# Weights times values in alternating column halves, and a 448/576 split of the subtraction, in a four-layer kernel

## Chip, core and metric

The kernel runs on one core of a Trainium2 chip. The metric is the device time of one execution in microseconds (us), as a median over several executions. The core has a matrix engine (TensorE, PE in the profile, with its weight loads in a row of their own, PEld), VectorE (DVE), ScalarE (ACT), GpSimd (POOL), and SyncE (SP), which issues DMAs. They run side by side and meet only at semaphores.

## The reference

Four layers act one after the other on x of shape (4, 1024, 128): a Mamba block, a mixture of experts, a differential attention, and a block with masked attention and experts. Only the third layer is touched. Per batch b it computes, for 8 heads with 64 value columns each:

```
dots = einsum('bhqd,bhkd->bhqk', q, k)          # 16 score maps, D = 32, two per head
attn_w = softmax(dots)
attn_w = attn_w[:, :, 0] - lam * attn_w[:, :, 1]  # one difference per head
attn = einsum('bhqk,bhkd->bhqd', attn_w, v)       # 64 value columns per head
attn = gamma * (attn / (rms + EPS)) * (1.0 - LAMBDA_INIT)
return attn.reshape(B, T, 512) @ Wout
```

T is 1024, so each head has two 1024x1024 maps in each of the 4 batches.

## The kernel before

The attention stage works in 256 units. Unit n is one block of 128 queries of one head: `unit(n)` gives batch b (64 units each), head group g (two heads, 16 units), query block i, and pp, which of the two heads. Two neighbouring units are a pair: the same queries, two heads. A pair's result is one 128x128 tile.

For one unit, two score maps of 128x1024 are made (`scores` with s = 0 and 1). On PE each is two f16 matmuls (L932) into a PSUM tile of its own, ps[0] or ps[1]. DVE takes the row maximum (L1090), and ACT the exponential with its row sum (L1017), into an SBUF buffer `P_of(n, s)`. The PSUM tile is then free for the next unit's map of the same s: PE waits for `a_ex(n - 1, s)`. Once a pair, `sums` makes the coefficients of the subtraction: a reciprocal on DVE (L1094), then two small POOL steps (L1147, L1151). `difference` computes z * coefficient + a in place: columns 0 to W on DVE (L1099), the others on POOL in two steps (L1156 multiply, L1159 add). W is 640 of 1024. `flip` transposes the difference in 8 chunks on PE (L943) into ps[2], and ACT copies it to SBUF as `DT[n % 2]` (L1024). `weigh` multiplies it by the values: 8 chunks, each with weights of 128x64 and a moving tile of 128x128 in f32 (L954), summed in PSUM partitions 64*pp to 64*pp + 64 of bank 6. PE executes each f32 product as two loads and two matmuls, so one `weigh` is 16 of each in the profile. When both heads of a pair are done, ACT copies the bank out (`gather`, L1030) and PE transposes it (`settle`, L960); DVE scales it (L1107).

All engines walk through one list, `ORDER`, made by `attention_order()`: its loop over n gives for each "slot" n what is put in line, and each engine takes what concerns it, in that order, never out of turn. Into these slots two more kinds of work are laid. Preparing pieces make the operands of the next head group (`op`: L914 on PE, L996 on ACT, L1084 on DVE; `v`: L919, L1004; `turn`, `norm`). Tail pieces `a0` to `a4` finish a batch whose last head group is being settled: root mean square (L1166, L1171 to L1175 on POOL, L1114 to L1123 on DVE) and output projection (L965 and L973 on PE). A batch's tail runs while the next batch's units go on. SP issues the DMAs that stack the operands (L892).

Of the kernel before, what the change touches and what calls it, by code (L numbers as in the profile page):

```python
# [8 lines left out]
F32 = mybir.dt.float32  # L9
# [3 lines left out]
ALU = mybir.AluOpType  # L13
ACT = mybir.ActivationFunctionType
# [90 lines left out]
def program(nc, d, out):  # L105
    ctx = ExitStack()
    with ctx:
# [16 lines left out]
        SEL = sb("sel", [128, 4096], BF16)  # L124
# [588 lines left out]

        N_UNITS, TL, W = 256, 4, 640
        s_wa, s_stack = sem("s_wa"), [[sem(f"s_stack{i}{j}") for j in range(2)] for i in range(2)]

        def unit(n):
            return n // 64, n // 16 % 4, n // 2 % 8, n % 2

        def attention_order():  # L720
# [47 lines left out]

            for n in range(N_UNITS + 8):
                if 0 <= n - 6 < N_UNITS and n % 2:  # L770
                    order.append(("gather", n - 6))
                if n < N_UNITS:
# [9 lines left out]
                if n < N_UNITS:  # L782
                    order.append(("scores", n, 1))
                if 0 <= n - 7 < N_UNITS and n % 2 == 0:
                    order.append(("settle", n - 7))
                    b, g, i, pp = unit(n - 7)
# [20 lines left out]
        t_axt, t_aop, t_av = tick("t_axt", NB, 2), tick("t_aop", NB, 4, 2, 2), tick("t_av", NB, 4, 2)  # L807
        t_as, t_at, t_aw, t_az = tick("t_as", N_UNITS, 2), tick("t_at", N_UNITS), tick("t_aw", N_UNITS), tick("t_az", PAIRS)
        t_a3, t_a4 = tick("t_a3", NB, 8), tick("t_a4", NB, 8)
# [6 lines left out]
        v_a1, v_a2 = tick("v_a1", NB, 8), tick("v_a2", NB, 8)  # L816
        p_ac, p_ad = tick("p_ac", PAIRS), tick("p_ad", N_UNITS)
        p_asq, p_arb, p_ax = tick("p_asq", NB, 8), tick("p_arb", NB, 8), tick("p_ax", NB)
# [31 lines left out]
        def ap2(x):  # L850
# [6 lines left out]
        V = [WB[:, 2048 + 1024 * i:3072 + 1024 * i].rearrange("p (j n) -> p j n", j=8) for i in range(2)]  # L857
        P_ = ([WB[:, 6144 + 1024 * i:7168 + 1024 * i] for i in range(3)] + [MA[:, 1024 * i:1024 * i + 1024] for i in range(3)]
              + [SEL[:, 2048 * i:2048 * i + 2048].bitcast(F32) for i in range(2)] + [WB[:, 5120:6144], BC[:, 0:2048].bitcast(F32)])
# [35 lines left out]
        def attention_pe(e):  # L895
            e.wait_ge(phase, 4)
            for p in ORDER:
# [37 lines left out]
                elif kind == "flip":  # L935
# [4 lines left out]
                    for k in range(8):  # L940
                        if 128 * k == W:
                            e.wait_ge(*p_ad.at(n))
                        x = e.transpose(ps[2][:, 128 * k:128 * k + 128], P_of(n, 0)[:, 128 * k:128 * k + 128], ident[:, :])  # L943
                    x.then_inc(*t_at.up(n))
                elif kind == "weigh":
                    n = p[1]
                    b, g, i, pp = unit(n)
                    e.wait_ge(*a_at.at(n))
                    if i == pp == 0:
                        e.wait_ge(*a_av.at(b, g, 1))  # L950
                    if pp == 0 and n:
                        e.wait_ge(*a_ag.at(n // 2 - 1))
# [23 lines left out]
        def attention_act(e):  # L976
# [3 lines left out]
            for p in ORDER:  # L980
# [17 lines left out]
                elif kind == "v":  # L998
# [3 lines left out]
                    if q >= 2 and h == 0:  # L1002
                        e.wait_ge(*t_aw.at(16 * q - 17))
                    e.activation(V[q % 2][:, 4 * h:4 * h + 4, :], bk.rearrange("p (j n) -> p j n", j=4), ACT.Copy,  # L1004
                                 scale=1.0).then_inc(*a_av.up(b, g, h))
                elif kind == "scores":
                    _, n, s = p
                    pp = n % 2
                    e.wait_ge(*v_amx.at(n, s))
                    if n >= 5:  # L1010
                        if s == 0:
                            e.wait_ge(*t_at.at(n - 5))
                        else:
                            e.wait_ge(*v_ad.at(n - 5))
                            e.wait_ge(*p_ad.at(n - 5))
                    L = L_of(n)
                    e.activation(P_of(n, s), ps[s][:, :], ACT.Exp, bias=L[:, 2 * s + pp:2 * s + pp + 1], scale=1.0,  # L1017
                                 accum_out=L[:, 4 + 2 * s + pp:5 + 2 * s + pp]).then_inc(*a_ex.up(n, s))
                elif kind == "flip":
                    n = p[1]  # L1020
                    e.wait_ge(*t_at.at(n))
                    if n >= 2:
                        e.wait_ge(*t_aw.at(n - 2))
                    e.activation(DT[n % 2], ps[2][:, :], ACT.Copy, scale=1.0).then_inc(*a_at.up(n))  # L1024
                elif kind == "gather":
                    m = p[1] // 2
                    e.wait_ge(*t_aw.at(2 * m + 1))
                    if m >= 2:
# [15 lines left out]
        def attention_dve(e):  # L1044
# [12 lines left out]
            for p in ORDER:  # L1057
# [33 lines left out]
                elif kind == "sums":  # L1091
                    n = p[1]
                    e.wait_ge(*a_ex.at(n, 1))
                    e.reciprocal(L_of(n)[:, 8:12], L_of(n)[:, 4:8]).then_inc(*v_ar.up(n // 2))  # L1094
                elif kind == "difference":
                    n = p[1]
                    e.wait_ge(*p_ac.at(n // 2))
                    a, z = P_of(n, 0), P_of(n, 1)
# [36 lines left out]
        def attention_pool(e):  # L1135
            e.wait_ge(phase, 4)
            for p in ORDER:
                kind = p[0]
                if kind == "norm" and p[2] == 1:
                    b = p[1]  # L1140
                    e.wait_ge(*v_ast[0].at(b))
                    rstd(e, st["m"]).then_inc(*p_ars[0].up(b))
                elif kind == "sums":
                    n = p[1]
                    L = L_of(n)
                    e.wait_ge(*v_ar.at(n // 2))
                    e.tensor_tensor(L[:, 12:14], L[:, 4:6], L[:, 10:12], ALU.mult).then_inc(*pool_own.up())  # L1147
                    if n == 1:
                        e.wait_ge(*v_lam.at(2))
                    e.wait_ge(*pool_own.now())  # L1150
                    e.tensor_scalar(L[:, 14:16], L[:, 12:14], lsc[:, 5:6], None, ALU.mult).then_inc(*p_ac.up(n // 2))  # L1151
                elif kind == "difference":
                    n = p[1]
                    a, z = P_of(n, 0), P_of(n, 1)
                    e.wait_ge(*p_ac.at(n // 2))
                    e.tensor_scalar(z[:, W:1024], z[:, W:1024], L_of(n)[:, 14 + n % 2:15 + n % 2], None, ALU.mult).then_inc(  # L1156
# [693 lines left out]
```

## Time and profile before

| | us |
|---|---|
| median of 3 runs (lowest to highest) | 3175.75 (3171.67 to 3178.06) |
| the profiled execution, its own time | 3170.2 |
| its span in the trace | 3168.4 |
| PE busy in the span | 2407.0 (76%) |
| DVE busy | 2311.8 (73%) |
| ACT busy | 1678.5 (53%) |
| POOL busy | 1263.5 (40%) |

The busy shares are over the whole program. The attention stage, from about 1289 us to 2500 us of the span, is a good third of it and has its own shares, which the rows below give by stretch. Matmul durations include the time through the array, so neighbouring ones overlap, and the distance between starts says more than a duration.

### The profile page before, as it was taken

How to read it: one execution, taken by the hardware profiler on the slowest of the kernel's cores; microseconds unless marked ns; L12 is line 12 of the kernel's file. 1: busy time of each engine (PE TensorE's matmuls, PEld its weight loads, DVE VectorE, ACT ScalarE, POOL GpSimd, SP SyncE). 2: the span in 40 equal slices, each digit the busy share in tenths (PEclk: the TensorE clock that was granted, in tenths of full speed). 3: DMA queues.
4: the chain of work that ended last, by engine and by line, in shares of the span. 5: the costliest groups of instructions: out<-in, count | busy, mean ns of one | idle time of the engine just before them, and what ended most of it. 6: DMA issues, size and time to landing. Idle time of an engine off the chain costs nothing.

```text
span 3168.4 us, 41094 instructions
## 1 busy us (share of the span) xinstructions
PE 2407.0 (76%) x14962; PEld 1690.2 (53%) x14962; DVE 2311.8 (73%) x4141; ACT 1678.5 (53%) x2552; POOL 1263.5 (40%) x1203
## 2 busy tenths in 40 slices
PE   3114776667676696899999999999999388667867
PEld 1002444344344564577777777776777366245635
DVE  3994798699599612688878878887888533874386
ACT  4223663665376242678777877787778124022402
POOL 0341143144124200365766576667667540114011
PEclk8556878888788898799999999999999789788978
DMA  3000000000000000100000100010000100000000
GB/s 99 0 0 0 0 1 1 1 1 1 1 1 1 1 1 14 41 21 21 24 21 21 28 21 21 24 29 21 21 21 1 40 1 1 0 14 1 1 0 14
DMA packets 32026, 41.96 MB, mean 13 GB/s; under 512 B 8897, under 2 KB 18130, under 8 KB 31442
## 3 DMA queue, kind: packets, MB, share of 16 engines
q1 hardware_dynamic: 31826, 39.34, 4.6%
q8 instruction: 120, 1.97, 0.3%
q14 instruction: 80, 0.66, 0.1%
HBM read 12.05 MB, written 2.10 MB: 4 GB/s over the span
## 4 chain that ended last, share of the span: by engine, by line
PE 46%; DVE 20%; issue 18%; POOL 11%; ACT 4%; SPq 1%; DMA 1%; POOLq 0%; DVEq 0%; ACTq 0%
PE ps L954 10%; PE ps L932 6%; PE ps L943 6%; POOL MA L379 5%; PE ps L710 3%; DVE MA L1090 3%; DVE MA L1410 3%; PE ps L914 2%; DVE lnb L265 2%; PE ps L1724 2%; PE ps L645 2%; PE ps L1711 2%; PE ps L647 1%; PE ps L646 1%; PE ps L1648 1%
## 5 line engine op out<-in xcount | busy, mean ns | idle before, releaser
L1090 DVE TENSOR_REDUCE MA<-ps 128x1 f32<-128x1024 f32 x512 | 623.1, 1220 | 190.4 <-PE ps L932 177.6
L379 POOL TENSOR_TENSOR MA<-MA,BIG 128x1024 f32<-128x1024 f32 x120 | 280.1, 2355 | 624.3 <-DVE BIG L350 624.3
L954 PE MATMUL ps<-MA,WB 128*64 128x128 f32 x4096 | 504.5, 277 | 0.0
L954 PEld LDWEIGHTS ps<-MA,WB 128*64 128x64 f32 x4096 | 442.8, 137 | 88.4 <-issue 87.4
L344 DVE TENSOR_TENSOR_SCAN BIG<-BIG 128x1024 f32<-128x1024 f32 x128 | 346.8, 2748 | 0.0
L932 PE MATMUL ps<-BIG 96*128 96x512 f16 x1024 | 312.6, 387 | 13.3 <-DMA BIG<-WB 4.9
L632 ACT ACTIVATE HR<-ps,b 128x512 f32<-128x512 f32 x288 | 191.5, 686 | 244.0 <-PE ps L647 243.0
L710 PEld LDWEIGHTS ps<-WB,HR 128*128 128x128 f32 x2304 | 305.8, 209 | 25.0 <-issue 8.7
L710 PE MATMUL ps<-WB,HR 128*128 128x128 f32 x2304 | 312.8, 294 | 0.0
L1017 ACT ACTIVATE WB<-ps,MA 128x1024 f32<-128x1024 f32 x206 | 229.5, 1114 | 149.3 <-DVE MA L1090 147.5
L497 PE MATMUL ps<-bc,sel 96*128 96x512 bf16 x256 | 108.2, 520 | 249.1 <-DVE BIG L350 190.7
L1024 ACT ACTIVATE MA<-ps 128x1024 f32<-128x1024 f32 x256 | 259.8, 1015 | 4.9 <-PE ps L943 4.9
L436 ACT ACTIVATE BIG<-MA,aneg 128x1024 f32<-128x1024 f32 x128 | 141.5, 1142 | 109.9 <-DVE BIG L344 105.8
L1017 ACT ACTIVATE MA<-ps,MA 128x1024 f32<-128x1024 f32 x153 | 170.6, 1115 | 44.8 <-DVE MA L1090 44.8
L497 PEld LDWEIGHTS ps<-bc,sel 96*128 96x128 bf16 x256 | 22.2, 113 | 302.2 <-DVE BIG L350 213.0
L1147 POOL TENSOR_TENSOR MA<-MA 128x2 f32<-128x2 f32 x128 | 25.0, 195 | 365.2 <-DVE MA L1094 365.2
L943 PE MATMUL ps<-ident,WB 128*128 128x128 f32 x1232 | 166.1, 279 | 5.6 <-POOL WB L1159 2.5
L943 PEld LDWEIGHTS ps<-ident,WB 128*128 128x128 f32 x1232 | 144.4, 144 | 44.4 <-DVE WB L1099 10.8
L645 PE MATMUL ps<-xT,WB 128*128 128x512 f16 x288 | 126.5, 439 | 52.4 <-ACT HR L632 48.3
L248 POOL TENSOR_SCALAR st_d<-st_d 128x8 f32<-128x8 f32 x16 | 4.3, 269 | 402.6 <-DVE st_d L260 402.5
L589 DVE SCALAR_TENSOR_TENSOR acc<-ps,g,acc 128x128 f32<-128x128 f32 x256 | 71.0, 337 | 123.2 <-PE ps L710 123.2
L340 DVE TENSOR_TENSOR BIG<-MA,ps 128x1024 f32<-128x1024 f32 x128 | 149.6, 1207 | 1.2 <-PE ps L497 1.2
(286 smaller groups left out, 5133.2 us busy)
## 6 DMA issues: line engine op xcount, KB each, us to landing
BIG<-BIG SPq DMA_DIRECT2D x192, 64.0 KB, 2.0
BIG<-WB SPq DMA_DIRECT2D x192, 64.0 KB, 2.0
WB<-w_dram SPq DMA_DIRECT2D x1, 2304.0 KB, 14.6
X<-x_dram SPq DMA_DIRECT2D x4, 512.0 KB, 12.5
HR<-w_dram SPq DMA_DIRECT2D x1, 2048.0 KB, 9.3
out_dram<-X SPq DMA_DIRECT2D x4, 512.0 KB, 3.2
WB<-wqkv_dram SPq DMA_DIRECT2D x1, 1536.0 KB, 6.1
WB<-w_dram SPq DMA_DIRECT2D x2, 512.0 KB, 8.2
```

The lines of the kernel that those rows point to most:

```text
L340: e.tensor_tensor(db[k][c], du[:, c, :], ps[0][:, :], ALU.mult).then_inc(*v_mtb.up(b, n, c))
L344: e.tensor_tensor_scan(db[k][c], da[k][c], db[k][c], 0.0, ALU.mult, ALU.add).then_inc(*v_mscan.up(b, n, c))
L379: e.tensor_tensor(yy[:, c, :], yy[:, c, :], db[n % 2][c], ALU.add).then_inc(*p_my.up(b, n, c))
L632: e.activation(hr[(4 * k + f) % 8], bank[4 + f % 2], ACT.Gelu, bias=small["b1"][:, PLAN[k][1], f:f + 1], scale=BACK).then_inc(*a_fg.up(b, ...
L645: e.matmul(o, w[0], x[0], start=first, stop=False)
L710: i = e.matmul(o, hr[(4 * kk + f) % 8][:, 128 * j:128 * j + 128], w2[:, x, f, :], start=f == 0 and x != 8, stop=f == 3)
L932: x = e.matmul(ps[s][:, 512 * h:512 * h + 512], stack[q % 2][0:96, 0, 2 * pp + s, 128 * i:128 * i + 128], stack[q % 2][0:96, 1, 2 * pp + s ...
L943: x = e.transpose(ps[2][:, 128 * k:128 * k + 128], P_of(n, 0)[:, 128 * k:128 * k + 128], ident[:, :])
L954: x = e.matmul(bank[6][64 * pp:64 * pp + 64, 0:128], V[(4 * b + g) % 2][:, k, 64 * pp:64 * pp + 64], DT[n % 2][:, 128 * k:128 * k + 128], ...
L1017: e.activation(P_of(n, s), ps[s][:, :], ACT.Exp, bias=L[:, 2 * s + pp:2 * s + pp + 1], scale=1.0, accum_out=L[:, 4 + 2 * s + pp:5 + 2 * s ...
L1024: e.activation(DT[n % 2], ps[2][:, :], ACT.Copy, scale=1.0).then_inc(*a_at.up(n))
L1090: e.tensor_reduce(L_of(n)[:, c:c + 1], ps[s][:, :], AX, ALU.max, negate=True).then_inc(*v_amx.up(n, s))
```

## The change

`weigh` no longer does one head after the other. It is now done for a pair in two pieces: piece 0 takes chunks 0 to 3 and piece 1 chunks 4 to 7, and within a piece each chunk is done for head 0 and then for head 1. The two heads' weights lie in different column halves of the array, and their results in different partitions of bank 6. Each piece still has 8 products (16 loads and 16 matmuls in the profile). Since a piece needs both heads' differences, it stands one or two slots later; `gather` and `settle` move one and two slots later, and `DT` has four buffers. These take over the memory of two of the ten P buffers; now the s = 0 maps have five and the s = 1 maps three, so the exponential of (n, 1) waits for the difference of n - 3 and no longer of n - 5. The subtraction is split at 448: DVE does 448 columns, POOL 576. The coefficients are made on DVE alone, the reciprocal and then one small fused step, which waits for the reciprocal by a semaphore.

```
-        N_UNITS, TL, W = 256, 4, 640
+        N_UNITS, TL, W = 256, 4, 448
...
-                if 0 <= n - 6 < N_UNITS and n % 2:
-                    order.append(("gather", n - 6))
+                if 0 <= n - 7 < N_UNITS and n % 2 == 0:
+                    order.append(("gather", n - 7))
...
-                if 0 <= n - 7 < N_UNITS and n % 2 == 0:
-                    order.append(("settle", n - 7))
+                if 0 <= n - 9 < N_UNITS and n % 2 == 0:
+                    order.append(("settle", n - 9))
...
-                if 0 <= n - TL - 1 < N_UNITS:
-                    order.append(("weigh", n - TL - 1))
+                if 0 <= n - 6 - n % 2 < N_UNITS:
+                    order.append(("weigh", (n - 6) // 2, n % 2))
...
-        DT = [MA[:, 3072 + 1024 * i:4096 + 1024 * i] for i in range(2)]
+        DT = ([MA[:, 3072 + 1024 * i:4096 + 1024 * i] for i in range(2)]
+              + [SEL[:, 2048 * i:2048 * i + 2048].bitcast(F32) for i in range(2)])
...
         def P_of(n, s):
-            return P_[(2 * n + s) % 10]
+            return P_[s][n % len(P_[s])]
...
-                    for k in range(8):
-                        x = e.matmul(bank[6][64 * pp:64 * pp + 64, 0:128], V[(4 * b + g) % 2][:, k, 64 * pp:64 * pp + 64],
-                                     DT[n % 2][:, 128 * k:128 * k + 128], start=k == 0, stop=k == 7)
-                    x.then_inc(*t_aw.up(n))
+                    for k in range(4 * half_, 4 * half_ + 4):
+                        for pp in range(2):
+                            x = e.matmul(bank[6][64 * pp:64 * pp + 64, 0:128], V[(4 * b + g) % 2][:, k, 64 * pp:64 * pp + 64],
+                                         DT[(2 * m + pp) % 4][:, 128 * k:128 * k + 128], start=k == 0, stop=k == 7)
+                    x.then_inc(*t_aw.up(m, half_))
...
-                    if n >= 5:
-                        if s == 0:
-                            e.wait_ge(*t_at.at(n - 5))
-                        else:
-                            e.wait_ge(*v_ad.at(n - 5))
-                            e.wait_ge(*p_ad.at(n - 5))
+                    if s == 0 and n >= 5:
+                        e.wait_ge(*t_at.at(n - 5))
+                    if s == 1 and n >= 3:
+                        e.wait_ge(*v_ad.at(n - 3))
+                        e.wait_ge(*p_ad.at(n - 3))
...
-                    e.reciprocal(L_of(n)[:, 8:12], L_of(n)[:, 4:8]).then_inc(*v_ar.up(n // 2))
+                    L = L_of(n)
+                    e.reciprocal(L[:, 8:12], L[:, 4:8]).then_inc(*v_ar.up(n // 2))
+                    if n == 1:
+                        e.wait_ge(*v_lam.at(2))
+                    e.wait_ge(*v_ar.at(n // 2))
+                    e.scalar_tensor_tensor(out=L[:, 14:16], in0=L[:, 4:6], scalar=lsc[:, 5:6], in1=L[:, 10:12], op0=ALU.mult,
+                                           op1=ALU.mult).then_inc(*v_ac.up(n // 2))
...
-                elif kind == "sums":
-                    n = p[1]
-                    L = L_of(n)
-                    e.wait_ge(*v_ar.at(n // 2))
-                    e.tensor_tensor(L[:, 12:14], L[:, 4:6], L[:, 10:12], ALU.mult).then_inc(*pool_own.up())
-                    if n == 1:
-                        e.wait_ge(*v_lam.at(2))
-                    e.wait_ge(*pool_own.now())
-                    e.tensor_scalar(L[:, 14:16], L[:, 12:14], lsc[:, 5:6], None, ALU.mult).then_inc(*p_ac.up(n // 2))
```

On PE, in two neighbouring slots in the middle of the stage, there stood this before (L932 scores, L943 flip, L960 settle, L954 weigh, x8 products):

```order
L932 MATMUL ps<-BIG 128x512 x2
L943 MATMUL ps<-ident,MA 128x128 x8
L932 MATMUL ps<-BIG 128x512 x2
L960 MATMUL ps<-ident,OS 128x128
L954 MATMUL ps<-MA,WB 64x128 x8
L932 MATMUL ps<-BIG 128x512 x2
L943 MATMUL ps<-ident,sel 128x128 x8
L932 MATMUL ps<-BIG 128x512 x2
L954 MATMUL ps<-MA,WB 64x128 x8
```

Now, with the lines moved by a few (L933, L944, L963, L957), and with a preparing piece (L915) in the row:

```order
L933 MATMUL ps<-BIG 128x512 x2
L944 MATMUL ps<-ident,bc 128x128 x8
L933 MATMUL ps<-BIG 128x512 x2
L963 MATMUL ps<-ident,OS 128x128
L957 MATMUL ps<-sel,WB 64x128 x8
L915 MATMUL ps<-xT,WB 128x512
L933 MATMUL ps<-BIG 128x512 x2
L944 MATMUL ps<-ident,WB 128x128 x8
L933 MATMUL ps<-BIG 128x512 x2
L957 MATMUL ps<-sel,WB 64x128 x8
```

The places of the weigh blocks between the scores are the same, and so is the count of 8 products in each; what is new is inside a block, where heads alternate. On DVE, one pair stood so before (L1090 maxima, L1094 reciprocal, L1107 scaling of a settled tile, L1099 difference):

```order
L1090 TENSOR_REDUCE MA<-ps 128x1
L1094 RECIPROCAL MA<-MA 128x4
L1090 TENSOR_REDUCE MA<-ps 128x1
L1107 TENSOR_TENSOR MA<-ps,MA 128x128
L1099 SCALAR_TENSOR_TENSOR WB<-WB,MA 128x640
L1090 TENSOR_REDUCE MA<-ps 128x1 x2
L1099 SCALAR_TENSOR_TENSOR WB<-MA,WB 128x640
```

and stands so now (L1092, L1097, L1115, L1107 in the same roles, L1101 the new small step):

```order
L1092 TENSOR_REDUCE MA<-ps 128x1
L1097 RECIPROCAL MA<-MA 128x4
L1101 SCALAR_TENSOR_TENSOR MA<-MA,lsc 128x2
L1092 TENSOR_REDUCE MA<-ps 128x1
L1115 TENSOR_TENSOR MA<-ps,MA 128x128
L1107 SCALAR_TENSOR_TENSOR WB<-MA,WB 128x448
L1092 TENSOR_REDUCE MA<-ps 128x1 x2
L1107 SCALAR_TENSOR_TENSOR bc<-MA,bc 128x448
```

One small step has come between the reciprocal and the second maximum, and the differences are narrower.

## Rows read from the trace of the kernel before

**Rows 1.** Busy time of each engine by stretch (us, and number of instructions)

```profile
1321.00:1530.00 209.00, 206.40 (x1470) 154.69 (x1469) 176.45 (x233) 171.37 (x288) 124.20 (x150) 1.00 0.10 25
...
1562.00:1634.00 72.00, 65.74 (x461) 50.72 (x460) 55.65 (x72) 51.85 (x90) 54.23 (x62) 0.98 0.09 23
1634.00:1732.00 98.00, 92.93 (x667) 71.51 (x665) 82.34 (x137) 72.25 (x126) 57.99 (x68) 1.00 0.07 17
1732.00:1828.00 96.00, 94.33 (x666) 70.53 (x667) 80.67 (x100) 80.47 (x136) 58.62 (x70) 1.00 0.12 28
```

**Rows 2.** Reciprocals (L1094, one a pair) in two stretches: DVE busy, number

```profile
1562.00:1634.00 72.00, 1.18 (x7) 0.98 0.09 23
1634.00:1732.00 98.00, 1.49 (x9) 1.00 0.07 17
```

**Rows 3.** The chain of waits from 1798 us: start, us, what

```profile
1800.04 1.89 PE ps L954 x16
1801.93 1.05 PE ps L914 x2
1802.98 0.43 PE ps L932 x2
1803.42 0.88 PE ps L943 x8
...
1806.62 0.54 PE ps L932 x2
...
1808.59 0.11 PE ps L960
```

**Rows 4.** Timeline of one pair: start, us, engine and instruction [idle before]

```profile
1799.96 1.23 DVE L1090 TENSOR_REDUCE MA<-ps 128x1 f32<-128x1024 f32 x1
1799.97 1.96 PE L954 MATMUL ps<-MA,WB 128*64 128x128 f32 x16
...
1803.46 2.53 DVE L1090 TENSOR_REDUCE MA<-ps 128x1 f32<-128x1024 f32 x2 [1.28 <-PE ps L932]
...
1804.71 1.11 ACT L1017 ACTIVATE WB<-ps,MA 128x1024 f32<-128x1024 f32 x1 [0.93 <-DVE MA L1090]
...
1805.82 1.02 ACT L1024 ACTIVATE MA<-ps 128x1024 f32<-128x1024 f32 x1
...
1806.72 1.11 ACT L1017 ACTIVATE WB<-ps,MA 128x1024 f32<-128x1024 f32 x1
...
1807.72 0.21 ACT L1017 ACTIVATION_READ_ACCUMULATOR WB<-ps,MA 128x1 f32 x1
...
1807.98 0.60 PE L932 MATMUL ps<-BIG 96*128 96x512 f16 x2
...
1808.63 1.23 DVE L1090 TENSOR_REDUCE MA<-ps 128x1 f32<-128x1024 f32 x1
```

**Rows 5.** Groups by shape, 1600 to 2200 us: busy us, mean ns, idle before

```profile
L954 PEld LDWEIGHTS ps<-MA,WB 128*64 128x64 f32 x2048 | 220.1, 137 | 44.4 <-issue 43.9
...
L1099 DVE SCALAR_TENSOR_TENSOR WB<-WB,MA 128x640 f32<-128x640 f32 x26 | 23.6, 906 | 2.7 <-POOL MA L1151 2.7
...
L914 PEld LDWEIGHTS ps<-xT,WB 128*128 128x128 f32 x64 | 9.5, 188 | 10.1 <-issue 4.8 <-DVE HR L1107 2.7 <-DVE MA L1107 2.7
```

**Rows 6.** POOL's groups by shape, 1828 to 1863 us (a batch's tail)

```profile
L1173 POOL TENSOR_TENSOR MA<-MA,half 128x8 f32<-128x8 f32 x3 | 5.5, 1837 | 0.2
L1166 POOL TENSOR_TENSOR MA<-HR 128x512 f32<-128x512 f32 x4 | 4.1, 1035 | 0.0
...
L1156 POOL TENSOR_SCALAR MA<-MA 128x384 f32<-128x384 f32 x2 | 2.5, 1242 | 0.1
...
L1159 POOL TENSOR_TENSOR MA<-MA 128x384 f32<-128x384 f32 x1 | 1.0, 998 | 0.1
...
L1151 POOL TENSOR_SCALAR MA<-MA,lsc 128x2 f32<-128x2 f32 x3 | 0.9, 296 | 0.3
L1147 POOL TENSOR_TENSOR MA<-MA 128x2 f32<-128x2 f32 x3 | 0.6, 197 | 2.3 <-DVE MA L1094 2.3
```

More of the change, by code:

```diff
@@ L767, in tail_piece @@
                     tails[0][2] = v
-            for n in range(N_UNITS + 8):
-                if 0 <= n - 6 < N_UNITS and n % 2:
-                    order.append(("gather", n - 6))
+            for n in range(N_UNITS + 11):
+                if 0 <= n - 7 < N_UNITS and n % 2 == 0:
+                    order.append(("gather", n - 7))
                 if n < N_UNITS:
@@ L783, in attention_order @@
                     order.append(("scores", n, 1))
-                if 0 <= n - 7 < N_UNITS and n % 2 == 0:
-                    order.append(("settle", n - 7))
-                    b, g, i, pp = unit(n - 7)
+                if 0 <= n - 9 < N_UNITS and n % 2 == 0:
+                    order.append(("settle", n - 9))
+                    b, g, i, pp = unit(n - 9)
                     if g == 3:
@@ L857, in program @@
         V = [WB[:, 2048 + 1024 * i:3072 + 1024 * i].rearrange("p (j n) -> p j n", j=8) for i in range(2)]
-        P_ = ([WB[:, 6144 + 1024 * i:7168 + 1024 * i] for i in range(3)] + [MA[:, 1024 * i:1024 * i + 1024] for i in range(3)]
-              + [SEL[:, 2048 * i:2048 * i + 2048].bitcast(F32) for i in range(2)] + [WB[:, 5120:6144], BC[:, 0:2048].bitcast(F32)])
+        P_ = [[WB[:, 6144 + 1024 * i:7168 + 1024 * i] for i in range(3)] + [WB[:, 5120:6144], BC[:, 0:2048].bitcast(F32)],
+              [MA[:, 1024 * i:1024 * i + 1024] for i in range(3)]]
         osl = [OS[:, 128 * i:128 * i + 128] for i in range(2)]
-        DT = [MA[:, 3072 + 1024 * i:4096 + 1024 * i] for i in range(2)]
+        DT = ([MA[:, 3072 + 1024 * i:4096 + 1024 * i] for i in range(2)]
+              + [SEL[:, 2048 * i:2048 * i + 2048].bitcast(F32) for i in range(2)])
         O_ = [MA[:, 5120:9216].rearrange("p (i n) -> p i n", i=8), HR[:, :].rearrange("p (i n) -> p i n", i=8)]
@@ L940, in attention_pe @@
                     for k in range(8):
-                        if 128 * k == W:
+                        if k == W // 128:
                             e.wait_ge(*p_ad.at(n))
@@ L945, in attention_pe @@
                 elif kind == "weigh":
-                    n = p[1]
[L947 to L952, printed above, removed]
-                    for k in range(8):
-                        x = e.matmul(bank[6][64 * pp:64 * pp + 64, 0:128], V[(4 * b + g) % 2][:, k, 64 * pp:64 * pp + 64],
-                                     DT[n % 2][:, 128 * k:128 * k + 128], start=k == 0, stop=k == 7)
-                    x.then_inc(*t_aw.up(n))
+                    _, m, half_ = p
+                    b, g, i, _ = unit(2 * m)
+                    if half_ == 0:
+                        e.wait_ge(*a_at.at(2 * m + 1))
+                        if i == 0:
+                            e.wait_ge(*a_av.at(b, g, 1))
+                        if m:
+                            e.wait_ge(*a_ag.at(m - 1))
+                    for k in range(4 * half_, 4 * half_ + 4):
[3 more added lines that the diff above has]
+                    x.then_inc(*t_aw.up(m, half_))
                 elif kind == "settle":
@@ L1002, in attention_act @@
                     if q >= 2 and h == 0:
-                        e.wait_ge(*t_aw.at(16 * q - 17))
+                        e.wait_ge(*t_aw.at(8 * q - 9, 1))
                     e.activation(V[q % 2][:, 4 * h:4 * h + 4, :], bk.rearrange("p (j n) -> p j n", j=4), ACT.Copy,
@@ L1021, in attention_act @@
                     e.wait_ge(*t_at.at(n))
-                    if n >= 2:
-                        e.wait_ge(*t_aw.at(n - 2))
-                    e.activation(DT[n % 2], ps[2][:, :], ACT.Copy, scale=1.0).then_inc(*a_at.up(n))
+                    if n >= 4:
+                        e.wait_ge(*t_aw.at(n // 2 - 2, 1))
+                    e.activation(DT[n % 4], ps[2][:, :], ACT.Copy, scale=1.0).then_inc(*a_at.up(n))
                 elif kind == "gather":
                     m = p[1] // 2
-                    e.wait_ge(*t_aw.at(2 * m + 1))
+                    e.wait_ge(*t_aw.at(m, 1))
                     if m >= 2:
```

9 lines of the change are left out of this document (4 added, 5 removed).

## The prediction

> **What bounds the kernel now.** I read the page's busy shares first, then only the attention stage, since nothing else is touched. Busy time by stretch [rows 1] shows PE at 206.4 of 209 us, at granted clock 1.00, in the first long regular stretch; DVE and ACT are at 84% and 82%, POOL at 59%. The stage has four sequences, one a batch. A batch's tail overlaps the next batch's start, and there no engine is full: 1562 to 1634 us has PE at 65.7 of 72, POOL at 54.2. The stretch after it, 1634 to 1732, is again near PE's limit, 92.9 of 98. The later sequences repeat this pattern, and the last has nothing left to prepare.
>
> The chain of waits [rows 3] says the same in detail. For pairs with a preparing piece it runs through PE without a gap: two weigh blocks of 1.89, one L914 of 1.05, scores of 0.43 and 0.54 twice each, two flips of 0.88, one settle of 0.11. The sum is 3.78 + 1.05 + 1.94 + 1.76 + 0.11 = 8.64 us, and the timeline [rows 4] has the second maximum of one pair at 1799.96 and of the next at 1808.63, 8.67 apart. So PE is full. But the same rows hold a second limit which is just as tight, and I think it decides this case. From the first maximum of the odd slot (1803.46) the work goes: exponential at 1804.71, the copy of the flip at 1805.82, the other exponential at 1806.72, its accumulator read until 1807.93, PE's scores at 1807.98, the second maximum at 1808.63. Every step starts as the one before it ends. These 5.17 us are a chain over DVE, ACT and PE that holds no weigh block.
>
> **The change, part by part.**
>
> *Weigh.* A block has 16 matmuls in 1.89 us, 0.118 each [rows 3]. A flip, with the full 128 columns of weights, takes 0.88 for 8, 0.110 each. So a product with 64 columns costs as much as one with 128: half the array stands idle. The trace of before holds no case of two column halves in neighbouring matmuls, so the overlap is to be bounded. Lower end: two halves fully side by side, 0.95 us. Upper end: none, 1.89. Between them I look at the loads. A load of 64 columns takes 137 ns and one of 128 columns 188 [rows 5], so 64 columns cost about 51 ns of streaming and the rest is latency; 16 loads in a row would need 0.82, less than 0.95, so loads alone don't forbid the overlap. But an engine that now wants two loads per matmul time has little spare, and some latency will show. I take 1.1 us, nearer the lower end, a choice: saving 0.79 per block.
>
> The Trainium skill, "TensorE: Matmul & The Clock Gate", section "Part 3: Packing small matmuls — row/col tiling", says that column tiles run at the same time and reports 2.38 times for three of them; by that ratio per tile (an estimate) two would give 1.59, a block of 1.19, and the total below would lose about 7 us of its gain. The same section says a load overlaps running matmuls only when the row group differs, which would speak against the change, since both halves use all rows. The trace disagrees for loads of one tile: the 137 ns loads fit 16 into a block of 1.89 us without adding to it.
>
> *What the saving is worth.* In an even slot the order is scores, flip, scores, settle, weigh, preparing piece, and then the next slot's scores; the rows of the order show that the change keeps this. From the second maximum at 1799.96 to the next slot's first at 1803.46 are 3.50 us, through the weigh block and L914; this part gets 0.79 shorter. Then comes the 5.17 chain, in which the second block of the pair is hidden. A pair with a preparing piece thus takes 3.50 − 0.79 + 5.17 = 7.88 instead of 8.67. The second block's saving is lost in this chain.
> A pair without one: PE's way would be 3.50 − 1.05 − 0.79 = 1.66, but DVE has a maximum, a settle scaling and a difference to do, some 2.0 us (1.23 as the row has it, and about 0.8 for the other two, narrowed). So 2.0 + 5.2 = 7.2, where PE's sum of before is 8.64 − 1.05 = 7.6 to 7.7; gain 0.5. In 8 pairs there are 6 with a piece (4 L914, 2 of L919): the mean gain is (6 × 0.79 + 2 × 0.5) / 8 = 0.72.
> Regular pairs: 209 us at 8.6 are 24 or 25, and each later sequence has 12 (96 us, [rows 1]); the last has about 7 pairs without any piece. 54 × 0.72 + 7 × 0.5 = 42 us. The stretch like 1634 to 1732 has 9 pairs [rows 2] and comes three times; it has output projections on PE besides, and I give it the same 0.72: 27 × 0.72 = 19 us. Together −61.
>
> *DVE.* The difference of 640 columns takes 0.906 mean [rows 5]; 192 fewer of 640 columns, if all but 0.2 scales, saves 0.2 twice a pair. The new small step with its wait for the reciprocal costs 0.15 to 0.3 (POOL's small steps take 0.2 and 0.3, [rows 6], and nearer rows there aren't). It sits between the two maxima, on the 5.17 chain's side branch. Net 0 to −0.2 per pair; I count 0. Behind that wait on DVE stands the second maximum, for which ACT waits, but ACT comes to it 2 us after the first.
>
> *POOL.* Each difference goes from 384 to 576 columns. Now 1.242 + 0.08 + 0.998 = 2.32 [rows 6]. With 0.2 fixed in each (the 2-column step takes 0.197) it becomes 1.76 + 0.08 + 1.40 = 3.24, in proportion 3.44. Per pair +1.8 to +2.2, and −0.75 for the two coefficient steps with their gaps. POOL then has about 6.5 to 6.9 per pair of 7.9: covered in regular stretches. The exponential of (n, 1) now waits for the difference of n − 3. Counted from the coefficients, the first difference is ready after 3.3 and wanted after about 6, the second after 6.6 and wanted after about 10: some 3 us of cover. If that cover goes, ACT stalls, and behind it the flip copies.
> In tails it is gone. There POOL also has 1.04 and 1.84 and two small steps, about 3.6 us with gaps per row block, next to each pair [rows 6]: 5.4 + 3.6 = 9.0 before, 6.5 + 3.6 = 10.1 and more after. About 12 pairs of each of three tails (4 before 1562, 7 in 1562 to 1634 [rows 2], and one) get 1.1 to 1.4 longer on POOL; POOL is 75% busy there, so I let half of it reach the end: 12 × 1.25 × 0.5 = 7.5, less 12 × 0.72 × 0.5 = 4.3 that PE gives: +3 each, +9, rounded to +8. The last tail has nothing to hide it: 4 pairs × 1.1, and it starts two slots later because settle moved: +12.
>
> *The rest.* The later gather, settle and V-buffer waits have whole slots of room; weigh of a pair waits for the second head's copy, made one slot before; SP's stacking is unchanged. Counted at 0; if the gather came late, PE's next first piece would stand, about 0.3 a pair.
>
> **The sum.** −61 + 8 + 12 = −41 us. The profiled execution has 3170.2 (span 3168.4), so 3129. It is 5.6 below the median of 3175.75; on the medians I forecast 3135 us.
>
> **The rivals.**
> *A, the chain loosens.* Overlap is full (0.95 to 1.0) and the 5.17 chain isn't binding, because a head start of one slot is carried along; the pair goes to what DVE needs, about 84% of 8.66, 7.2. Then 54 × 1.46 + 7 × 0.5 + 27 × 1.2 = 115, less 20 for tails: 3081. For it: DVE idles 1.28 before 1803.46. Against it: every start in the chain touches an end.
> *B, slower: the halves don't overlap.* PE runs products in turn whatever their columns, the block stays 1.89, and no regular pair gains. The tails pay in full: 12 × 1.25 × 0.5 × 3 = 22, and 12 at the end: 3175.75 + 34 = 3210. It decides from a block of about 1.63 us upwards, since the 61 us of gain shrink in proportion and 20 must be paid. The skill's sentence on row groups would be this case. For it: no row shows overlap; each matmul is paced by its 128 moving rows.
> *C, POOL takes the bound.* Its steps are stretched beside DVE's wider use of the same memory and take 4 us per difference: 8 us a pair. Then the regular pairs gain about 0.6, 88 × 0.6 = 53 in all, and the tails pay 12 × 2.4 × 0.5 × 3 = 43 and 18: 3184. For it: POOL's steps of one shape differ in length. Against: means are near the shortest.
>
> **Chances and range.** Forecast 0.48 (3105 to 3160), A 0.20, B 0.20, C 0.12. From them: faster by over 0.2% (what a measurement of this kernel can tell, about 6 us) 0.72, with a little of C; same 0.07; slower 0.21. The range runs from 3075, just under A, to 3200, which leaves out most of B: 3075 to 3200.
>
> **What would show it.** The weigh row: 16 matmuls in about 1.2 us, against 1.96. Steady pairs 7.9 apart with a piece and 7.2 without. PE no longer full, 85 to 90% in regular stretches. POOL at 576 columns 1.76 and 1.40, over 80% busy; ACT waiting for POOL only in tails, and the last stretch after the final unit longer. I am wrong if the block keeps its length, if starts in the 5.17 chain draw apart, or if ACT waits for L1159's successor in steady pairs.

## The result and the profile after

The changed kernel takes 3193.74 us in the median (3187.35 to 3198.83, five runs), the kernel before 3176.47 beside it (3171.67 to 3179.14): ratio 1.0055, 95% interval 1.0038 to 1.0071. It is slower by half a per cent, where I had forecast 3135. The profiled execution has a span of 3195.1, against 3168.4.

The page's busy rows and its chain, of the changed kernel:

```profile
PE 2257.7 (71%) x14962; PEld 1491.2 (47%) x14962; DVE 2346.0 (73%) x4269; ACT 1679.1 (53%) x2552; POOL 1426.6 (45%) x947
...
PE 32%; DVE 31%; issue 19%; POOL 12%; ACT 5%; SPq 1%; DMA 1%; POOLq 0%; ACTq 0%; DVEq 0%
```

PE is busy for 149 us less, yet the kernel is not faster. The stretches that answer to [rows 1] (PE, PEld, DVE, ACT, POOL busy, granted clock, DMA):

```profile
1321.00:1530.00 209.00, 174.36 (x1458) 112.71 (x1458) 182.95 (x254) 169.69 (x288) 153.12 (x98) 0.98 0.10 24
...
1562.00:1634.00 72.00, 56.83 (x470) 39.60 (x471) 57.31 (x81) 52.94 (x92) 65.72 (x50) 0.98 0.09 23
1634.00:1732.00 98.00, 78.38 (x630) 53.64 (x628) 83.54 (x127) 73.09 (x125) 73.05 (x50) 0.93 0.07 17
1732.00:1828.00 96.00, 78.17 (x632) 51.88 (x632) 79.42 (x121) 71.55 (x122) 67.48 (x43) 0.95 0.10 25
```

In the first stretch PE went from 206.4 to 174.4 of 209, and DVE from 176.5 to 183.0. The timeline of a steady pair with a preparing piece answers to [rows 4]:

```profile
1802.62 1.22 DVE L1092 TENSOR_REDUCE MA<-ps 128x1 f32<-128x1024 f32 x1
...
1802.63 1.09 PE L957 MATMUL ps<-sel,WB 128*64 128x128 f32 x16
...
1803.77 0.28 DVE L1115 TENSOR_TENSOR HR<-ps,MA 128x128 f32<-128x128 f32 x1
...
1804.10 1.12 PE L915 MATMUL ps<-xT,WB 128*128 128x512 f32 x2 [0.38 <-DVE HR L1115]
...
1805.70 2.53 DVE L1092 TENSOR_REDUCE MA<-ps 128x1 f32<-128x1024 f32 x2 [1.06 <-PE ps L933]
...
1807.69 1.40 POOL L1158 TENSOR_TENSOR WB<-WB,MA 128x576 f32<-128x576 f32 x1
...
1808.15 1.42 DVE L1107 SCALAR_TENSOR_TENSOR WB<-MA,WB 128x448 f32<-128x448 f32 x1
...
1811.56 1.22 DVE L1092 TENSOR_REDUCE MA<-ps 128x1 f32<-128x1024 f32 x1
```

Three things are to be seen. The weigh block has 16 matmuls in 1.09 us, where it had 1.96: the column halves do run side by side. PE then waits for DVE's L1115: the scaling of the settled tile reads bank 7, into which the preparing piece L915 is to write, and on DVE it stands behind a maximum of 1.22 us. And the difference L1107 of the odd slot takes 1.42 us for 448 columns, where 640 took 0.9; it begins while POOL's add L1158 runs and ends 0.48 after it. The chain of waits has both, and repeats every 9.06 us:

```profile
1811.64 1.13 DVE MA L1092
1812.78 0.21 DVE HR L1115
1812.98 0.04 issue
1813.03 1.12 PE ps L915 x2
1814.15 0.43 PE ps L933 x2
1814.59 0.88 PE ps L944 x8
1815.46 0.45 PE ps L933 x2
1815.91 0.02 issue
1815.93 1.23 DVE MA L1092
1817.16 1.47 DVE WB L1107
1818.63 0.60 DVE BIG L1086
1819.23 1.13 DVE MA L1092
```

No weigh block is left in it, and no step of ACT either. (I had written that the engines meet only at semaphores; these two steps, which no semaphore joins, show that VectorE and GpSimd do not.)

Where the time went by stretch is read from the reciprocals, one a pair. The 40th and the 52nd, which bound the middle of the second sequence, first of the kernel before, then of the changed one:

```profile
1642.96 0.17 DVE L1094 RECIPROCAL MA<-MA 128x4 f32<-128x4 f32 x1
...
1757.56 0.17 DVE L1094 RECIPROCAL MA<-MA 128x4 f32<-128x4 f32 x1
```

```profile
1642.27 0.16 DVE L1097 RECIPROCAL MA<-MA 128x4 f32<-128x4 f32 x1
...
1771.03 0.17 DVE L1097 RECIPROCAL MA<-MA 128x4 f32<-128x4 f32 x1
```

These 12 pairs went from 114.6 to 128.8 us. The same stretches of the third and fourth sequence lost 14.1 and 12.1, so 40 in all; everything else between the first and the last reciprocal gained 17.5 together; behind the last one 4.0 were lost. 40.4 − 17.5 + 4.0 is the 27 by which the spans differ.

The twelve pairs do not hold the same work in both kernels. Settle stands two slots later, and with it every tail piece of the batch: by `ORDER`, 15 tail pieces fall between these two reciprocals where there were 12, and 27 into the twelve pairs before them where there were 30. Those earlier pairs gained 3.8, 3.2 and 5.7 us in the three sequences. Of the 14.2, 14.1 and 12.1 lost, 9.6, 10.1 and 11.9 lie in the last three pairs, where the kernel before has no tail piece left.

Two more things are seen in the same stretch: what PE waited for (us in all, times, longest), and the busy times with the granted clock (the third number from the end), each first of the kernel before, then of the changed one:

```profile
PE ps L914 <- DVE HR L1107: 2.2, 2, 1.9
...
PE ps L973 <- DVE WB L1084: 0.8, 1, 0.8
```

```profile
1642.96:1757.56 114.60, 107.86 (x761) 81.45 (x760) 97.58 (x158) 86.66 (x149) 69.60 (x80) 1.00 0.09 22
```

```profile
PE ps L915 <- DVE HR L1115: 9.5, 8, 4.9
PE ps L976 <- DVE BIG L1086: 6.3, 3, 2.4
```

```profile
1642.27:1771.03 128.76, 99.87 (x774) 68.49 (x774) 105.77 (x172) 88.51 (x151) 88.73 (x60) 0.91 0.08 19
```

With the smaller rows, PE's waits for DVE at the spare bank were 4.6 us and are 21.0. Half of the 21.0 is not the wait for the scaling: the projection pieces of the tail (L968, L976) wait for L1086, DVE's last step of an odd slot, which stands behind the difference. And the granted clock, 1.00 before, is now 0.91 (0.91 and 0.90 in the other two sequences), so that part of the stretch ran at the lower of the two levels, 1.2 GHz. One such place, behind a wait of 3.02 us:

```profile
1715.81 1.03 PE L933 MATMUL ps<-BIG 96*128 96x512 f16 x2 [3.02 <-ACT bc L1019]
...
1719.53 1.98 PE L957 MATMUL ps<-MA,WB 128*64 128x128 f32 x16
```

The weigh block takes 1.98 there instead of 1.09. The PE steps that stand in the chain of waits at such lengths add up to some 8 to 10 us more than the same steps at clock 1.00 (an estimate, from the chain between these two reciprocals). No run holds the clock fixed, so what it is worth is not shown; e9 below loses 33 us in the three stretches at 0.97, so it is not the whole of the 40.

### The profile page after: what moved, and what is told of

Read it like the earlier page. It is cut to its first block, busy times and chain, and to the rows that moved or that the text cites. A ratio compares the mean times of both kernels' runs of the same rounds, so it can differ in the third digit from the quotient of the medians.

```text
span 3195.1 us, 40966 instructions
## 1 busy us (share of the span) xinstructions
PE 2257.7 (71%) x14962; PEld 1491.2 (47%) x14962; DVE 2346.0 (73%) x4269; ACT 1679.1 (53%) x2552; POOL 1426.6 (45%) x947
## 4 chain that ended last, share of the span: by engine, by line
PE 32%; DVE 31%; issue 19%; POOL 12%; ACT 5%; SPq 1%; DMA 1%; POOLq 0%; ACTq 0%; DVEq 0%
DVE MA L1092 10%; POOL MA L379 5%; PE ps L933 4%; PE ps L944 4%; PE ps L710 3%; DVE MA L1409 3%; DVE WB L1107 3%; POOL MA L1155 2%; PE ps L915 2%; DVE lnb L265 2%; PE ps L1723 2%; PE ps L645 2%; PE ps L1710 2%; PE ps L646 1%; PE ps L647 1%
## 5 line engine op out<-in xcount | busy, mean ns | idle before, releaser
L1092 DVE TENSOR_REDUCE MA<-ps 128x1 f32<-128x1024 f32 x512 | 623.1, 1220 | 189.0 <-PE ps L933 180.7
L1155 POOL TENSOR_SCALAR MA<-MA 128x576 f32<-128x576 f32 x256 | 454.3, 1775 | 257.8 <-DVE MA L1101 256.8
L933 PE MATMUL ps<-BIG 96*128 96x512 f16 x1024 | 325.0, 400 | 52.1 <-ACT WB L1019 31.5
L1158 POOL TENSOR_TENSOR WB<-WB,MA 128x576 f32<-128x576 f32 x205 | 293.1, 1430 | 17.1
L1019 ACT ACTIVATE MA<-ps,MA 128x1024 f32<-128x1024 f32 x256 | 286.2, 1118 | 22.9 <-POOL WB L1158 12.3
L944 PE MATMUL ps<-ident,WB 128*128 128x128 f32 x1640 | 233.1, 287 | 40.1 <-ACT MA L1026 12.5
L944 PEld LDWEIGHTS ps<-ident,WB 128*128 128x128 f32 x1640 | 197.7, 148 | 112.6 <-issue 48.2
L1107 DVE SCALAR_TENSOR_TENSOR WB<-MA,WB 128x448 f32<-128x448 f32 x205 | 188.5, 919 | 0.0
L933 PEld LDWEIGHTS ps<-BIG 96*128 96x128 f16 x1024 | 83.4, 101 | 146.7 <-ACT WB L1019 50.0
## 6 DMA issues: line engine op xcount, KB each, us to landing
X<-x_dram SPq DMA_DIRECT2D x4, 512.0 KB, 12.7
```

The lines of the kernel that those rows point to most:

```text
L933: x = e.matmul(ps[s][:, 512 * h:512 * h + 512], stack[q % 2][0:96, 0, 2 * pp + s, 128 * i:128 * i + 128], stack[q % 2][0:96, 1, 2 * pp + s ...
L1092: e.tensor_reduce(L_of(n)[:, c:c + 1], ps[s][:, :], AX, ALU.max, negate=True).then_inc(*v_amx.up(n, s))
L1107: e.scalar_tensor_tensor(out=a[:, 0:W], in0=z[:, 0:W], scalar=L_of(n)[:, 14 + n % 2:15 + n % 2], in1=a[:, 0:W], op0=ALU.mult, op1=ALU.add) ...
L1158: e.tensor_tensor(a[:, W:1024], a[:, W:1024], z[:, W:1024], ALU.add).then_inc(*p_ad.up(n))
```

## The experiments

Two theories. **Theory 1, the collision:** DVE's difference and POOL's add, which both read two operands in SBUF, hold each other up, and the change puts them beside each other. **Theory 2, the bank:** with a short weigh block PE waits for the scaling that frees the spare bank. A third was that POOL is simply overloaded. The clock and the moved tail pieces have no experiment of their own. Each kernel was timed beside the kernel before on the same chip; its ratio to that is given.

**e1_split640: the changed kernel, split back at 640.**

```
-        N_UNITS, TL, W = 256, 4, 448
+        N_UNITS, TL, W = 256, 4, 640
```

> The changed kernel with the split back at 640 columns on VectorE and 384 on GpSimd, all else as changed. Theory 1 (collision: VectorE's difference and GpSimd's add, which both read two operands in SBUF, shut each other out, and the wide share puts the add beside the difference of the odd slot): that difference falls from 1.4 to 1.5 us to about 0.9 to 1.1 in steady pairs although it has more columns, pairs with an op piece fall from 9.05 to about 8.5 to 8.7, and the kernel takes 3150 to 3170. Theory 2 (only the wait of PE for the spare bank counts): the difference gets longer by 0.2 and nothing else changes, so 3195 to 3215.

3167.02 us, ratio 0.9974 (0.9964 to 0.9984). Steady pairs with a piece take 8.38. In the same slot the wider difference takes less time than the narrow one did:

```profile
1808.75 1.00 POOL L1158 TENSOR_TENSOR WB<-WB,MA 128x384 f32<-128x384 f32 x1
...
1809.89 0.88 DVE L1107 SCALAR_TENSOR_TENSOR WB<-MA,WB 128x640 f32<-128x640 f32 x1
```

POOL's add is over before the difference begins. So the new split alone costs 27 us in this kernel; without it the rest of the change is slightly faster than before.

**e2_before448: the kernel before, split at 448** (same edit from 640, with the flip's wait for POOL's half put at chunk 3).

> The kernel before with only the split moved to 448/576. Theory 1: the odd slot's difference is stretched here too, to over 1.2 us, but PE has the weigh blocks of 1.89 beside it, so steady pairs stay near 8.7 to 9.0, and the tails pay for GpSimd's longer steps: 3185 to 3210. If the split were harmless and only the new order costs: 3170 to 3180.

3213.10 us, ratio 1.0125 (1.0109 to 1.0140), a little above what was expected: steady pairs alternate between 8.00 and 9.47. The split costs 39 us without anything else of the change.

**e3_in_turn: four chunks of one head, then four of the other.**

```
-                    for k in range(4 * half_, 4 * half_ + 4):
-                        for pp in range(2):
+                    for pp in range(2):
+                        for k in range(4 * half_, 4 * half_ + 4):
```

> The changed kernel with the two heads in turn inside a piece (four chunks of head 0, then four of head 1), all else as changed. If the overlap of the column halves is what made the block 1.02 us, the block goes back to about 1.9 and pairs with an op piece, whose chain holds one block partly hidden behind the scaling, get 0.3 to 0.5 longer: 3210 to 3235. If something else shortened the block, nothing changes: 3194.

3188.28 us, ratio 1.0041 (1.0028 to 1.0055). My expectation was wrong on both counts. The block did not go back to 1.9:

```profile
1803.51 1.58 PE L957 MATMUL ps<-sel,WB 128*64 128x128 f32 x16
```

And 0.5 us more per block cost nothing; steady pairs are at 9.05 as in the changed kernel, since PE would only have waited for the bank: in the steady pair L915's wait for L1115 is 0.38 us in the changed kernel and gone here. Why blocks of four and four take 1.58 and not 1.96 no run here settles.

**e4_settle_first: settle ahead of the slot's second scores.**

```
+                if 0 <= n - 9 < N_UNITS and n % 2 == 0:
+                    order.append(("settle", n - 9))
                 if n < N_UNITS:
                     order.append(("scores", n, 1))
                 if 0 <= n - 9 < N_UNITS and n % 2 == 0:
-                    order.append(("settle", n - 9))
                     b, g, i, pp = unit(n - 9)
```

> The changed kernel with settle put ahead of the slot's second scores, all else as changed. Theory 2 (PE waits for VectorE's scaling to free the spare bank, behind a 1.2 us maximum): the scaling now stands ahead of that maximum, the wait of L915's successor vanishes, steady op pairs get about 0.3 shorter and the middle stretches too: 3165 to 3180. Theory 1 alone: within 5 us of 3194.

3118.73 us, ratio 0.9825 (0.9811 to 0.9838). That is 75 us below the changed kernel, far more than the wait alone, and below what I had expected. A steady pair takes 7.5 to 7.6 (the first of each four still 9.06):

```profile
1782.15 0.67 DVE L1108 SCALAR_TENSOR_TENSOR WB<-MA,WB 128x448 f32<-128x448 f32 x1
1782.50 1.59 POOL L1159 TENSOR_TENSOR WB<-WB,MA 128x576 f32<-128x576 f32 x1
...
1784.81 0.28 DVE L1116 TENSOR_TENSOR HR<-ps,MA 128x128 f32<-128x128 f32 x1
...
1785.52 1.12 PE L916 MATMUL ps<-xT,WB 128*128 128x512 f32 x2
```

L916 waits for nothing in these pairs. And since the slots are shorter, the difference comes 0.35 us before POOL's add and takes 0.67; it is the add that is stretched, 1.59 for 1.40, and it is not in the chain of waits. I read the two theories as joined, the bank's wait having delayed the difference into the add; but e4 moves two things at once, and only the collision is taken away by itself, in e10. In the stretch between the 40th and 52nd reciprocal the projections still wait for L1086's successor, 8.6 us in all: e4 cures only the scaling's wait.

**e5_settle_split640: both edits, e4's order and e1's split.**

> Settle ahead of the second scores and the split at 640/384, all else as changed. If the collision of the two subtraction halves costs in the e4 order too, the wider difference costs 0.2 twice a pair on VectorE but tails lose GpSimd's 1.05 a pair: 3095 to 3125, near e4's 3119. If the collision is avoided at 448 only by luck of phase and comes back at 640, pairs with an op piece go from 7.5 to over 8 and the kernel to 3130 to 3150.

3125.58 us, ratio 0.9853 (0.9838 to 0.9868). In e4's order the split matters little, 7 us, where it was worth 27. The time is that of my first case, near e4's, but the pairs went over 8, as in the second: steady pairs 8.04, shorter pairs in the tails. Against e1 settle's place is worth 41 us here.

**e6_settle_serial: e4 with a whole head in each piece, no halves side by side.**

```
-                    for k in range(4 * half_, 4 * half_ + 4):
-                        for pp in range(2):
+                    for pp in (half_,):
+                        for k in range(8):
```

> e4's order, with each piece one whole head of 8 chunks (piece 0 head 0, piece 1 head 1), so that no two column halves stand side by side; all else as in e4. If the alternation is worth its 0.8 to 0.9 us per block once the bank's wait is gone, pairs with an op piece go from 7.5 to 8.4 to 8.7 and the kernel from 3119 to 3160 to 3185. If the order of settle alone made the gain, it stays within 10 of 3119.

3195.61 us, ratio 1.0069 (1.0056 to 1.0083): 77 us more than e4, the alternation's worth once the bank's wait is gone, and more than I had expected. The block is back at 1.89. Of the steady pair's 1.5 us (9.05 for 7.5) it explains 0.87; for the rest I take the collision, which is back with the longer slots (that the slots' length brings it back is argued, not tested). Two lines of the timeline and one of the chain:

```profile
1378.65 1.40 POOL L1159 TENSOR_TENSOR bc<-bc,MA 128x576 f32<-128x576 f32 x1
...
1378.77 1.77 DVE L1108 SCALAR_TENSOR_TENSOR bc<-MA,bc 128x448 f32<-128x448 f32 x1
```

```profile
1372.91 1.89 PE ps L958 x16
```

**e7_before_settle: the kernel before with settle first** (e4's edit).

> The kernel before with settle put ahead of the slot's second scores, nothing else. PE is full there, and its block of 1.89 already hides the wait for the scaling: within 8 us of 3174. If settle's place were a gain of its own whatever the weigh block, 3130 to 3160.

3166.87 us, ratio 0.9985 (0.9976 to 0.9994). Settle's place is worth 6 us here and 75 in the changed kernel. The two kernels differ in more than the block's length: with the long block in the changed kernel (e9 against e6) it is worth 19 by the medians, with e9's runs 14 us apart, and with the short block at the old split (e1 against e5) 41. So both the short block and the new split make it dear.

**e8_one_operand: POOL's add reads one operand.**

```
-                    e.tensor_tensor(a[:, W:1024], a[:, W:1024], z[:, W:1024], ALU.add).then_inc(*p_ad.up(n))
+                    e.tensor_scalar(a[:, W:1024], a[:, W:1024], 1.0, None, ALU.mult).then_inc(*p_ad.up(n))
```

> The changed kernel with GpSimd's add (two operands in SBUF) made a step with one operand, a copy by a factor of 1; it leaves the z part of 576 columns out of the difference, so the output is not the reference's. The step itself gets longer, about 1.7 for 1.4. Theory 1 (two-operand steps shut each other out): VectorE's difference of 448 columns takes 0.67 in every slot, pairs with an op piece go from 9.05 to about 8.3, and the kernel to 3150 to 3175 in spite of the longer step. If any step of GpSimd stretches it, or if the wait has another cause, it stays at 1.4 and the kernel at 3195 or more.

3163.06 us, ratio 0.9969 (0.9957 to 0.9981), 31 us below the changed kernel though POOL's step is longer. But theory 1 as I had put it holds only in part:

```profile
1364.16 1.65 POOL L1158 TENSOR_SCALAR WB<-WB 128x576 f32<-128x576 f32 x1
1364.25 1.04 DVE L1107 SCALAR_TENSOR_TENSOR WB<-MA,WB 128x448 f32<-128x448 f32 x1
```

The difference still takes 1.04 and not 0.67 when it begins beside this one-operand step, and the pair 8.55, not 8.3. Two operands on both sides is the costly case, but not the only one; how long each holds the difference up is in the last section.

**e9_serial: the changed kernel with e6's edit.**

> The changed kernel with each piece one whole head of 8 chunks, so no two column halves side by side, settle where the change has it, all else as changed. The settle-first pair of runs put the alternation at 77 us. Here the wait for the scaling already covers part of the block (the piece starts the wait anyway): theory 2 expects pairs with an op piece at 9.05 plus 0.4, 3205 to 3225; if the alternation were worth its full 0.87 in this order too, 3240 or more.

3214.13 us, ratio 1.0113 (1.0098 to 1.0129). In the changed kernel's own order the alternation is worth 20 us, a quarter of the 77 it is worth with settle first. Its steady pairs are at 9.06, as with the short block: there I had expected 0.4 more. The loss lies in the other pairs, and 6 us of it behind the last reciprocal.

**e10_early_difference: the changed kernel with the odd slot's difference ahead of its second scores.**

```
+                if 0 <= n - 2 < N_UNITS and n % 2:
+                    order.append(("difference", n - 2))
                 if n < N_UNITS:
                     order.append(("scores", n, 1))
...
-                if 0 <= n - 2 < N_UNITS:
+                if 0 <= n - 2 < N_UNITS and n % 2 == 0:
                     order.append(("difference", n - 2))
```

> The changed kernel with the difference of each odd slot put ahead of that slot's second scores, so that VectorE does it 1.2 us sooner, before GpSimd begins its add; same work, output the reference's. Theory 1 as one of phase: the odd slot's difference falls from 1.4 to 1.5 us to 0.68, ScalarE is busy until then anyway, pairs with an op piece fall from 9.05 to 8.2 to 8.4, 3150 to 3170. If what costs is the load of GpSimd and not the meeting of the two steps: 3190 to 3200.

3142.04 us, ratio 0.9903 (0.9889 to 0.9918), 52 us below the changed kernel with the same work on every engine, and a little below my range:

```profile
1372.28 0.68 DVE L1109 SCALAR_TENSOR_TENSOR bc<-MA,bc 128x448 f32<-128x448 f32 x1
...
1373.12 1.40 POOL L1160 TENSOR_TENSOR bc<-bc,MA 128x576 f32<-128x576 f32 x1
```

Difference and add no longer meet, the pair takes 8.25, and POOL's load, which is the same, is not the cause. PE's wait for the scaling, up to 0.4 us a pair, is still there, so the collision costs by itself. Between the 40th and 52nd reciprocals of the three sequences 29 of the 40 us come back, with the granted clock at 0.94 to 0.97.

**e11_both: e4 and e10 together.**

> Settle first and the early difference together. In e4's order the two steps hardly meet in steady pairs, so little is left there (7.5 to 7.6); the pairs of 8.5 and 9.1 and the middle stretches, where they still meet, should shorten: 3100 to 3115. If the second maximum, now 0.7 later, holds ScalarE up, 3120 to 3135.

3120.01 us, ratio 0.9829 (0.9816 to 0.9841), no different from e4, where I had expected 3100 to 3115. The middle stretches are 10 us shorter, but steady pairs take 7.72 for 7.5, as if the later second maximum took back what is won elsewhere; that it is the maximum is not shown.

**e12_coef_gpsimd: e4 with the two coefficient steps on POOL again.**

> e4 with the coefficients made on GpSimd as before (two small steps), all else as e4. VectorE is spared about 0.3 a pair, GpSimd gets 0.75 more and starts its steps about 0.4 later, which moves the add further behind the odd slot's difference: steady pairs 7.4 to 7.5, tails 0.75 a pair longer, 3120 to 3135. If the new small step on VectorE was a cost of the change on the chain: below 3112.

3163.33 us, ratio 0.9962 (0.9950 to 0.9975): 45 us more than e4, far above what I expected. Steady pairs are only 0.2 longer (7.69); the time goes into the tails and into the last pairs without a piece (7.90 for 6.89), both in this window of 50 us at the end of the stage:

```profile
2400.00:2450.00 50.00, 35.76 (x301) 22.70 (x299) 36.13 (x47) 32.33 (x54) 47.58 (x41) 0.92 0.00 1
```

POOL is busy for 47.6 of the 50 us, and most of its multiplications there take 2.1 to 2.2 us for 1.73. In e4's order the new small step on DVE is therefore no cost but a part of the change that pays.

## Why the prediction was wrong

**PE is full now, and a second chain of 5.17 us is as tight.** Right in the main: the steady pair changed from a bound on PE to one over DVE and PE, and the second block's saving was lost. But it is DVE, not ACT, that decides it: the 5.17 us chain kept its length up to PE's scores (1810.23 − 1805.70 = 4.53, before 4.52), and only its last step, the second maximum, came late, because DVE was not free.

**The weigh block at 1.1.** Right: 1.09 in the timeline, 1.02 in the chain of e4. The Trainium skill's sentence in "TensorE: Matmul & The Clock Gate", section "Part 3: Packing small matmuls — row/col tiling", by which a load overlaps running matmuls only when the row group differs, would have spoken against a gain; the trace disagrees with it for column halves: 16 loads and 16 matmuls in 1.09 us over the same rows.

**"This part gets 0.79 shorter."** Wrong, the first step that failed. I put the part from the second maximum to the next slot's first at 3.50 − 0.79 = 2.71. It took 3.08 (1802.62 to 1805.70). I had written that gather and settle have "whole slots of room" and counted them at 0, but looked only at who waits for the tile, and not at who waits for its bank. The wait of L915 for L1115, 0.38 us, had lain behind the block of 1.89: with the long block back (e9) it falls from 15.6 to 2.5 us in all between 1330 and 1530 us. e4 moved it away; e7 shows that it cost little in the kernel before.

**"DVE: net 0."** Wrong, the second and costlier step. I scaled the difference by its columns, 0.2 less. In the odd slot it took 1.42 to 1.47, and the part that I had at 5.17 took 5.86 (1805.70 to 1811.56). 2.71 + 0.37 and 5.17 + 0.69 make the 8.94 of that pair, instead of 7.88. The 0.69 is read from DVE's starts, first before, then now:

```profile
1805.91 0.87 DVE L1099 SCALAR_TENSOR_TENSOR sel<-sel,MA 128x640 f32<-128x640 f32 x1
...
1806.70 0.68 DVE L1084 SCALAR_TENSOR_TENSOR BIG<-ps,BIG 128x512 f16<-128x512 f32 x1
...
1808.43 0.17 DVE L1094 RECIPROCAL MA<-MA 128x4 f32<-128x4 f32 x1
```

```profile
1809.49 0.68 DVE L1086 SCALAR_TENSOR_TENSOR BIG<-ps,BIG 128x512 f16<-128x512 f32 x1
...
1811.22 0.16 DVE L1097 RECIPROCAL MA<-MA 128x4 f32<-128x4 f32 x1
...
1811.42 0.22 DVE L1101 SCALAR_TENSOR_TENSOR MA<-MA,lsc 128x2 f32<-128x2 f32 x1
```

From the difference's start to the next step's it is 1.34 for 0.79, 0.55 more; from the reciprocal to the second maximum, with the new small step between, 0.34 for 0.20, 0.14 more. The small step, too, was on this path and not on a side branch. I had the collision as rival C, but on POOL's side, as stretched POOL steps that would make POOL the bound; it was DVE's step that was stretched. e1, e8 and e10 show it by three different edits, worth 27, 31 and 52 us.

**"The stretch like 1634 to 1732 gains 0.72 a pair," and the regular pairs as well.** Wrong. The nine pairs of such a stretch (from the 40th reciprocal) lost 8.8 us over the three sequences, where −19 was forecast. The pairs counted as regular were to give −42 and took about 27 more, 31.6 of that in the three pairs behind each such stretch. Two things were put at nothing here. The tails of the first three batches end two pairs later, since settle moved; I had counted that for the last tail alone. And the sum takes every PE step at its length of before, where the granted clock of these stretches fell from 1.00 to 0.91. The difference's greater length goes into these pairs too, since DVE's last step of the slot stands behind it and projections wait for that step. e10 gives 29 of the 40 us back; how the other 11 divide between clock, moved pieces and bank is open. Even e4 doesn't gain there against the kernel before (115.8 us between the 40th and 52nd reciprocal, against 114.6, at clock 0.96).

**Tails +20.** Wrong, and on the other side. The twelve pairs from the 28th reciprocal on, and their like, got 12.7 us shorter in all, where +8 was forecast, helped by three fewer tail pieces in each; behind the last reciprocal 4.0 were lost, where +12 was forecast for the last tail. Only POOL's steps came as computed (1.73 and 1.40 for 1.76 and 1.40). **Pairs without a piece at 7.2.** Right: 7.10.

**The rivals.** The sign was B's, but not its mechanism, since the halves do overlap. Its price was good: without overlap, in the changed kernel's order, e9 has 3214 us, where B said 3210. That the time fell inside the range at all was luck: the range had been drawn wide enough for C and the edge of B. A, in which the pair comes near 7.2, was nearer than it looked: e4 has 7.5, though 3119 us and not 3081.

## What to carry to other kernels

When a step that an engine spends its time in gets short, ask which waits had lain under it, the wait for a shared buffer's release above all; moving one entry of the order (a transposition on PE with its scaling on DVE) was worth 6 us in the kernel before, 75 in the changed one, and 19 there with the long block back. Don't scale VectorE's two-operand steps by their width without looking where GpSimd's two-operand steps lie: moving work to GpSimd can lengthen what is left. The changed kernel is half a per cent slower or nearly two per cent faster by the place of that one entry, so a split between two engines is to be measured again after each change of order.

## What the runs showed of the hardware that I had not expected

- Two column halves of 64 in alternating f32 matmuls of 128 moving rows begin every 54 ns ((1.09 − 0.27) / 15, with 0.27 the duration of one), against 112 for one half; loads of 137 ns each kept up, 16 in 0.85 us. With four products of each half in turn it was 87 ns ((1.58 − 0.27) / 15), between the two.
- VectorE's two-operand difference of 448 columns takes 0.67 us alone. Begun 0.01 to 1.15 us after GpSimd's two-operand add of 576, it ended 0.47 to 0.50 us behind the add's end in all 483 such places of the traces, however late it began: 1.42 us when 0.46 late, 1.77 when 0.12 late. With 640 columns beside an add of 384 it was 0.67 to 0.69 behind. Most of the difference's own time thus comes after the add.
- Begun 0.04 us or more before the add, the difference kept its 0.67 in every place, and the add was stretched: 1.41 for 1.40 with 0.66 of lead, 1.59 with 0.36, 1.90 with 0.04. The step that began first kept its time, down to a lead of about 0.03 us, where it went either way.
- GpSimd's one-operand steps of 576 columns (the multiplication, and e8's copy) hold the difference up as well, but not to their end: begun 0.04 to 0.50 us after one, it ended 0.48 to 0.53 us before that step's end (231 places); begun 0.55 or more after it, it took 0.67 to 0.69. This is why e8 has 1.04.
- The granted clock was 0.91 between the 40th and 52nd reciprocals, where PE was busy for 99.9 of 128.8 us with waits of up to 4.9 us, and 1.00 in the next 64 us, where it was busy for 55.0 with waits of at most 1.2. At the lower level a weigh block took 1.98 us for 1.09 and a flip 1.71 for 1.04.
